# Moving the clips of the ternary weights, dropping one run of dummy matmuls, and adding the residual in two rounded parts

## The reference

```
x = x + cross_attention(layernorm(x), ctx_512)      # 16 heads, 4096 keys
x = x + self_attention(layernorm(x))                # 16 heads of 32, 256 keys
x = x + ffn(x)
# ffn, with quantised activations and ternary weights:
weight_quant(w) = clip(round(w * s), -1, 1) / s     # s = 1 / mean|w|
act_quant(h)    = clip(round(h * q), -128, 127) / q # q = 127 / max|h| of the token
h = silu(bitlinear(x, w1)) * bitlinear(x, w3)       # 512 -> 1408
ffn = bitlinear(h, w2)                              # 1408 -> 512
```

## Time and profile before

| what | value |
|---|---|
| median of three runs | 553.34 us (552.72 to 554.07) |
| profiled execution | 552.99 us |
| its span | 551.2 us |
| busy: PE, DVE, ACT, POOL | 525.1, 450.3, 364.7, 152.1 us |
| chain that ended last, by engine | PE 74%, DVE 11%, DMA 6%, ACT 5% |
| granted TensorE clock over the span | 1.00 |

### The profile page before, as it was taken

The page is one execution under the profiler, slowest core; times in us unless marked ns, Lnnn a source line. Parts: engine busy times, 40 slices in busy tenths (PEclk is TensorE's granted clock), DMA queues, the critical chain, the costliest instruction groups (busy, mean ns, idle before and its releaser), DMA issues.

```text
span 551.2 us, 10020 instructions
## 1 busy us (share of the span) xinstructions
PE 525.1 (95%) x3831; PEld 352.3 (64%) x3835; DVE 450.3 (82%) x650; ACT 364.7 (66%) x445; POOL 152.1 (28%) x202
## 2 busy tenths in 40 slices
PE   6989998799999999999999999999998999998996
PEld 3757663366666766666767666666777886454443
DVE  3354995999999999999999999999998933569686
ACT  2125435887886788688688688688779614995442
POOL 2357963002103202202202102112100301696500
PEclk9999999999999999999999999999999999999999
DMA  8999288999999999999999999999999968700001
GB/s 303 347 357 314 110 134 255 234 202 194 196 211 194 201 202 196 212 211 204 208 204 194 204 202 196 198 208 198 200 203 188 173 278 345 312 1 1 1 2 38
DMA packets 288350, 107.93 MB, mean 196 GB/s; under 512 B 276928, under 2 KB 278464, under 8 KB 286912
## 3 DMA queue, kind: packets, MB, share of 16 engines
q1 hardware_dynamic: 288320, 107.54, 89.7%
HBM read 37.79 MB, written 0.52 MB: 70 GB/s over the span
## 4 chain that ended last, share of the span: by engine, by line
PE 74%; DVE 11%; DMA 6%; ACT 5%; issue 2%; SPq 1%; ACTq 0%; DVEq 0%
PE ps L679 17%; PE ps L681 9%; PE ps L661 8%; PE ps L663 8%; PE ps L662 8%; PE ps L712 4%; DMA pT<-split 3%; DVE rows L1301 3%; PE ps L723 3%; DMA keys<-ctxT 2%; DVE split L1273 2%; PE ps L789 2%; PE ps L734 2%; PE ps L629 1%; PE ps L631 1%
## 5 line engine op out<-in xcount | busy, mean ns | idle before, releaser
L679 PE MATMUL ps<-pT,VH 128*128 128x256 f16 x1024 | 195.1, 273 | 2.1 <-DMA pT<-split 2.0
L681 PE MATMUL ps<-pT,VL 128*128 128x128 f16 x1024 | 182.0, 219 | 0.0
L1301 DVE TENSOR_SCALAR_CACHE_REDUCE rows<-ps,qback 128x1024 f32<-128x1024 f32 x128 | 163.6, 1280 | 17.3 <-PE ps L663 16.9
L1053 ACT ACTIVATE split<-rows,rz 128x2048 f16<-128x2048 f32 x64 | 124.6, 1994 | 67.1 <-DVE rz L1241 67.0
L1273 DVE SCALAR_TENSOR_TENSOR split<-rows,rz,split 128x2048 f16<-128x2048 f32 x64 | 150.2, 2349 | 2.9 <-ACT split L1053 2.1
L679 PEld LDWEIGHTS ps<-pT,VH 128*128 128x128 f16 x1024 | 100.2, 98 | 42.6 <-DMA pT<-split 4.5
L1039 ACT ACTIVATE rows<-rows,negm 128x2048 f32<-128x2048 f32 x64 | 127.2, 1988 | 0.2 <-DVE negm L1306 0.2
L681 PEld LDWEIGHTS ps<-pT,VL 128*128 128x128 f16 x1024 | 100.2, 98 | 26.8
L542 POOL TENSOR_TENSOR ctx_c<-acc 128x128 f32<-128x128 f32 x32 | 27.4, 856 | 292.9 <-ACT acc L1028 292.9
L661 PE MATMUL ps<-KH,qcur 128*128 128x512 f16 x256 | 97.1, 379 | 3.3 <-DVE rows L1301 3.3
L663 PE MATMUL ps<-KH,qcur 128*128 128x512 f16 x256 | 97.0, 379 | 0.0
(11 more groups left out here) (187 smaller groups left out, 622.7 us busy)
## 6 DMA issues: line engine op xcount, KB each, us to landing
w_sb<-w SPq DMA_DIRECT2D x3, 2816.0 KB, 16.1
wq_sb<-wq SPq DMA_DIRECT2D x4, 1024.0 KB, 8.4
wo_sb<-wo SPq DMA_DIRECT2D x16, 256.0 KB, 5.2
wkcq_sb<-wkcq SPq DMA_DIRECT2D x4, 768.0 KB, 9.8
keys<-ctxT SPq DMA_DIRECT2D x8, 256.0 KB, 8.9
stage<-ctxT SPq DMA_DIRECT2D x16, 128.0 KB, 9.1
stage<-kcos SPq DMA_DIRECT2D x8, 256.0 KB, 9.3
stage<-ksin SPq DMA_DIRECT2D x8, 256.0 KB, 9.7
```

The lines of the kernel that those rows point to most:

```text
L679: nc.tensor.matmul(bank(6 + r % 2, 0, 256), VH[:, 4 * b + k, :], p.rearrange("p x q -> p (x q)"), start=(b == 0 and k == 0), stop=False)
L681: last = nc.tensor.matmul(bank(6 + r % 2, 0, 128), VL[:, 4 * b + k, :], p[:, 0, :], start=False, stop=(b == 7 and k == 3))
L1053: nc.scalar.activation(split[:, split_slot(r, half), :, 0, :], rows[:, k, half * 2048:(half + 1) * 2048].rearrange("p (b k) -> p b k", k=1 ...
L1301: nc.vector.tensor_scalar(rows[:, k, c * 1024:(c + 1) * 1024], ps[:, score_bank(s) * 512:(score_bank(s) + 2) * 512], qback[:, r // 2:r // ...
```

## The change

Five edits, all in the hand-written orders.

1. VectorE's clips of w1 and w3 move from behind the maxima of units 4 and 5 to behind the second `context_out` (v = 5). Its clip of w2 goes.
2. GpSimd does its first pass over w2 before its wait for the two clips, and the second pass behind it. So this wait stands between the two passes.
3. GpSimd clips w2 itself, in the same eight pieces. It waits for both quantised token tiles (`h2b_done, TT`), does pieces 0 to 5, then its share of tile 0's `hmid`, then pieces 6 and 7, then its share of tile 1's `hmid`. TensorE's product with w2 waits piece by piece for `w2clip_done`.
4. The ten dummy matmuls ahead of the first quantised transposes go.
5. GpSimd splits x2 into a part rounded to the f32r format and the rounded remainder, and copies the identity into f32r; TensorE adds both parts by f32r products in place of one f32 product. No DMA is added or moved.

```diff
+        x2hi = at("x2hi", A + 22 * KB, [128, TT, DM], f32r)
+        x2lo = at("x2lo", A + 26 * KB, [128, TT, DM], f32r)
+        identr = at("identr", A + 30 * KB, [128, 128], f32r)
...
                 nc.gpsimd.tensor_tensor(x_sb[:, t, :], x_sb[:, t, :], h1[:, t, :], ALU.add).then_inc(x2_done, 1)
+                if t == 0:
+                    nc.gpsimd.tensor_copy(identr[:, :], ident[:, :]).then_inc(identr_done, 1)
+                pool.wait_ge(x2_done, t + 1)
+                nc.gpsimd.tensor_copy(x2hi[:, t, :], x_sb[:, t, :]).then_inc(x2hi_done, 1)
+                pool.wait_ge(x2hi_done, t + 1)
+                nc.gpsimd.tensor_tensor(x2lo[:, t, :], x_sb[:, t, :], x2hi[:, t, :].bitcast(f32), ALU.subtract)\
+                    .then_inc(x2lo_done, 1)
...
             weight_round(1, w3_sb, w3b)
+            weight_magic(2, w2_sb)
             pool.wait_ge(wclip_done, 2)
-            weight_magic(2, w2_sb)
             weight_round(2, w2_sb, w2b)
+            def last_clips(first, end):
+                for k in range(first, end):
+                    part = slice(k * DK * FF // WPIECES, (k + 1) * DK * FF // WPIECES)
+                    pool.wait_ge(wround_done, WPIECES * 2 + k + 1)
+                    nc.gpsimd.tensor_scalar(w2b[:, part], w2b[:, part], 1.0, -1.0, ALU.min, ALU.max).then_inc(w2clip_done, 1)
+            pool.wait_ge(h2b_done, TT)
+            last_clips(0, 6)
             for t in range(TT):
...
                     .then_inc(hmagic_done, 1)
+                if t == 0:
+                    last_clips(6, WPIECES)
...
-                pe.wait_ge(x2_done, t + 1)
-                nc.tensor.matmul(bank(6 + t), ident[:, :], x_sb[:, t, :], start=True, stop=False)
+                pe.wait_ge(identr_done, 1)
+                pe.wait_ge(x2lo_done, t + 1)
+                nc.tensor.matmul(bank(6 + t), identr[:, :], x2hi[:, t, :], start=True, stop=False)
+                nc.tensor.matmul(bank(6 + t), identr[:, :], x2lo[:, t, :], start=False, stop=False)
...
-            keep_busy(10, 2)
             quantised_transposes(0)
...
-                    pe.wait_ge(wclip_done, 3)
                     pe.wait_ge(gate_done, TT)
...
+                        if t == 0:
+                            pe.wait_ge(w2clip_done, -(-(c + 1) * DM // (DK * FF // WPIECES)))
...
-                if v in (2, 3):
-                    clip(v - 2, (w1b, w3b)[v - 2])
                 if v in (3, 5, 7):
                     context_out(v // 2 - 1)
+                if v == 5:
+                    clip(0, w1b)
+                    clip(1, w3b)
             context_out(FG - 1)
-            clip(2, w2b)
```

More of the change, by code:

```diff
@@ L292, in program @@
         wclip_done = sem("wclip_done")
+        w2clip_done = sem("w2clip_done")
+        identr_done = sem("identr_done")
+        x2hi_done = sem("x2hi_done")
+        x2lo_done = sem("x2lo_done")
         win_in = sem("win_in")
```

## The result

The changed kernel takes 549.37 us (median of six runs, 548.93 to 549.86); the kernel before, run beside it, 552.75. The ratio is 0.9933, with a 95% interval of 0.9920 to 0.9945: faster by 0.7%. The profiled execution took 549.50 us (before 552.99), span 547.7.

What follows compares the result with a forecast made beforehand. Bound by TensorE's products, later by its waits for VectorE's w1 clip, nine dummies and the hidden part's quantisation. -2.7 - 0.45 - 1.35 + 1.5 = -3.0 us, so 550.3 us; own range 549.6 to 550.9, with rivals 548.5 to 551.4.

Steps and rivals of the forecast that it cites:

- Step 1: VectorE's clips leave units 4 and 5, so maxima come earlier and TensorE's stalls before later transposes shrink: -2.7 us.
- The cover named for the clips: Third division starts 0.8 us late, yet its results precede the W_out products by 0.5 us or more; otherwise up to 0.8.
- Step 2: Residual on TensorE: two f32r products replace tile 0's f32 product with the identity, saving 0.45 us.
- The aside: GpSimd's new operations may hold up VectorE's last layernorm steps and first rotation by 0 to 1.3 us each; taken as 0.
- Step 3: Without dummies TensorE starts tile 0's quantised transposes sooner behind h2b, all of it on the path: -1.35 us.
- Step 4: GpSimd's w2 clips: pieces 6 and 7 shut VectorE out at the end of tile 0's quantisation: +1.5 us.
- the prediction's own sign of being wrong: VectorE's L1534 write at 1.04 us in tile 0, where some 2.5 was expected there or in L1530.
- The reading of the w1 clip: VectorE's w1 clip took 3.45 us because it stood still through GpSimd's stream, past the ends of two pieces.
- first rival's lower case: VectorE gets in between GpSimd's w2 clip pieces but loses one turn: 0.75 us, 549.6; chance 0.22 for the whole rival.
- that rival's sum: The forecast's terms with one lost VectorE turn, 0.75 us, in place of the 1.5 for GpSimd's w2 clips.
- The clock rival: Without dummies TensorE's clock falls over the w1 products: 2.7 us more, 553.0, or 555.5 if lasting; chance 0.05.

Runs made afterwards that it cites:

- clips_early: Changed kernel with VectorE's clips of w1 and w3 back behind the maxima of units 4 and 5, GpSimd's new order kept; 560.55 us, ratio 1.0119.
- the probes: Two runs of the changed kernel with two unread 768-column VectorE clips added, amid GpSimd's f32 passes and bf16 clips, source types swapped; read for durations only.
- f32_pieces: Changed kernel whose GpSimd pieces 6 and 7 of w2 read the f32 source with add and min, without the lower clip; 550.65 us, ratio 0.9939.
- w2_vector: Changed kernel in which VectorE clips w2 whole behind its last division and GpSimd clips nothing; 554.01 us, ratio 0.9999.

## Why the prediction was right, and where not

**Step 1, right in size and by its mechanism.** Predicted -2.7, found -2.69. Both clips at 1.62 us, GpSimd idle at the gate, the first two stalls gone, unit 7's wait still ScalarE's copy; clips_early shows the loss when the clips stand where GpSimd streams. The cover named for the clips held: the third division started late and W_out's products followed without a pause at the place.

**Step 2, right.** Predicted -0.45, found -0.39 and, with the edit undone, 0.40. No row showed the 0.05 counted for the switch of type; beside the two products' 0.46 the pair took 0.10 more, 0.56 in all. The aside also held: GpSimd's new operations stretched VectorE's last layernorm steps at no cost. Timeline of DVE, kernel after:

```profile
464.02 1.11 DVE L1405 TENSOR_TENSOR nt<-rs,ve 128x2 f32<-128x2 f32 x1
```

This two-element step took 0.16 before; now it waits for GpSimd's subtraction. TensorE's transposes, from 468.33, did not wait.

**Step 3, right.** Predicted -1.35; found -1.39 in the change and -1.34 alone.

**Step 4, right in its place, wrong in its size.** Predicted +1.5, found +0.59 (0.57 by undoing it). The pieces took the 0.75 us estimated, their end met VectorE's wide step as worked out, and pieces 6 and 7 were what VectorE lost time to. But the prediction's own sign of being wrong came: the write of 768 columns took 1.04 us as before and not 2.5, and the loss fell on the write of 640 behind it. What failed is the sentence "By the w1 clip, VectorE stays shut out until the stream ends". The reading of the w1 clip was sound (10.09 us in clips_early, 9.01 and 8.87 in the probes), but it belongs to GpSimd's f32 passes. It does not carry over to GpSimd's bf16 clips, which let VectorE in after one piece. The first rival's lower case, one lost turn, came true: its price was 0.75 against the 0.59 found. The Trainium skill's rule (SBUF — State Buffer, "Who interferes with whom") of one instruction and then the other fits here (0.59 and the probes' 0.66 and 0.86 us). It does not fit the f32 passes, nor f32_pieces, where VectorE was done 1.46 us before the GpSimd instruction.

**The figure came nearer than its terms.** For the profiled pair the forecast was -3.0 us and that rival's sum -3.75. The changed stretch gained 3.89, and the 0.41 lost ahead of it, which no step held, left 3.49: by luck of the two executions it hid nearly half of step 4's error. The median, 549.37, lies below the forecast's own 549.6 to 550.9. The stated range held because the rival had been given weight in it.

**The clock rival did not occur, but my argument against it was too strong.** The pause before the transposes was the 1 us foreseen, and the clock over them 1.00; nor did it fall behind the two shorter waits of 0.59 and 0.46 us for the hidden part. Yet "idle stretches of 1.61 and 2.00 us left the clock granted in full" rested on one execution: the like 2.00 us cost the clock in after. Step 3 is borne out for the pauses that it left: in all eleven profiles with 0.62 to 1.02 us at that place the transposes ran at a clock of 1.00. With 3.66 us there, w2_vector paid 2.3 us; nothing between was measured.

**What stays open:** which property of GpSimd's operation decides between shutting out and taking turns, what one turn is (the piece in after, less than the piece in f32_pieces), and why one 2.00 us pause loses the clock and its like doesn't.

## What to carry to other kernels

A blocking figure between VectorE and GpSimd belongs to the operation that GpSimd ran when it was read: before it is used for another operation, find that one in a trace or measure it, and give the range both ends. Put a long VectorE operation into a gap that a wait of GpSimd guarantees, not beside its stream. Before dummies go, work out the pause that TensorE is left with, and read the clock behind such pauses in more than one execution.

## What the runs showed of the hardware that I had not expected

- A VectorE clip of 768 columns took 9.01 and 8.87 us amid GpSimd's f32 passes, but 0.66 and 0.86 us amid its bf16 clips.
- GpSimd's TENSOR_SCALAR with add and min, f32 to bf16, took 2.56 and 2.87 us for 704 columns; with add and mult, f32 to bf16, 0.78 (5.97 for eight, which overlap a little); with min and max on bf16, 0.77.
- After the same 2.00 us pause the clock was 1.00 in one execution and 0.50 in another.
- A VectorE step on 128 x 2 values with two inputs took 1.11 us for 0.16 when it met GpSimd's subtraction.
